# Two batches around a self-attention, staged one behind the other, with the bf16 parts of keys and queries split by GpSimd

## The reference

```python
x = x + _L0_xattn_ref(_layernorm(x, axis=-1), ctx_1024, mask, ...)
x = x + _L0_ffn_ref(_layernorm(x, axis=-1), ...)
...
x = x + _L2_xattn_ref(_layernorm(x, axis=-1), ctx_1024, ...)
x = x + _L2_ffn_ref(_layernorm(x, axis=-1), ...)

def _L0_ffn_ref(hidden_states, ...):     # L2: rmsnorm, no biases, no causal mask
    resid = hidden_states
    x = layer_norm(hidden_states, ln1_w, ln1_b)
    q, k, v = (split(x @ w + b) for each)          # 16 heads of 8
    scores = jnp.where(causal, q @ k.T / sqrt(8), neg)
    ctx = softmax(scores) @ v
    hidden = resid + (ctx @ o_w + o_b)
    xt = layer_norm(hidden, ln2_w, ln2_b)
    logits = xt @ router_w                          # top 2 experts of 16 (L2: of 8)
    return hidden + combine(experts(xt))
```

## Time and profile before

| | us |
|---|---|
| median of 3 runs | 1254.61 (1251.87 to 1260.2) |
| profiled execution, time | 1259.82 |
| profiled execution, span | 1257.6 |
| TensorE busy | 958.8 (76%) |
| VectorE busy | 589.2 (47%) |
| ScalarE busy | 437.1 (35%) |
| GpSimd busy | 218.4 (17%) |

### The profile page before, as it was taken

One profiled execution on the slowest core, in us unless ns is written; L12 is line 12 of the kernel. 1 busy time (PEld: TensorE's weight loads), 2 busy tenths in 40 slices (PEclk: granted clock), 3 DMA queues, 4 the chain that ended last, 5 costly groups with the idle time before them and its releaser, 6 DMA issues. The chain is left out here.

```text
span 1257.6 us, 15487 instructions
## 1 busy us (share of the span) xinstructions
PE 958.8 (76%) x5556; PEld 645.7 (51%) x5561; DVE 589.2 (47%) x1312; ACT 437.1 (35%) x761; POOL 218.4 (17%) x243
## 2 busy tenths in 40 slices
PE   5872599833664638999778925999699988869998
PEld 3661244423653526677647811232266676756776
DVE  4867445351225462311766667576244446632111
ACT  2331155501331203343343310577432233424443
POOL 0334010005033200000372340001000011431100
PEclk9996589965996868999888965799889988989999
DMA  8001511001730000110000006020001111110111
GB/s 343 1 1 48 128 40 40 7 29 39 209 110 9 1 0 1 38 46 17 26 1 1 2 9 167 20 58 2 1 13 38 38 35 51 51 34 18 34 33 34
DMA packets 33264, 55.71 MB, mean 44 GB/s; under 512 B 3697, under 2 KB 25398, under 8 KB 32817
## 3 DMA queue, kind: packets, MB, share of 16 engines
q1 hardware_dynamic: 32176, 52.88, 13.8%
q0 software_dynamic: 1024, 1.98, 0.6%
HBM read 44.81 MB, written 9.96 MB: 44 GB/s over the span
## 5 line engine op out<-in xcount | busy, mean ns | idle before, releaser
L2089 PE MATMUL psum<-xT_all,wexp 128*128 128x512 f32 x400 | 185.1, 608 | 1.3 <-issue 0.7
L1380 DVE TENSOR_REDUCE arena<-psum 128x2 f32<-128x1024 f32 (+3 forms) x128 | 127.6, 1022 | 85.8 <-PE psum L1917 49.9
L949 ACT ACTIVATE arena<-psum 128x512 f32<-128x512 f32 (+3 forms) x256 | 115.8, 515 | 74.9 <-PE psum L1930 37.6
L697 POOL TENSOR_TENSOR rstd<-var,held 128x8 f32<-128x8 f32 (+2 forms) x24 | 51.9, 2180 | 415.8 <-DVE var L1148 392.1
L2089 PEld LDWEIGHTS psum<-xT_all,wexp 128*128 128x128 f32 x400 | 74.6, 196 | 79.1 <-issue 73.2
L1914 PE MATMUL psum<-arena 72*128 72x512 bf16 (+3 forms) x256 | 85.1, 406 | 25.2 <-DMA arena<-parts_q 19.1
L2104 PEld LDWEIGHTS psum<-wexp,arena 128*128 128x128 f32 x800 | 94.2, 192 | 16.2 <-issue 14.4
L1849 PE MATMUL psum<-values_out_all,arena 128*128 128x128 f32 x560 | 78.5, 289 | 26.5 <-ACT arena L921 26.2
L727 POOL TENSOR_TENSOR arena<-arena,small 128x616 f32<-128x616 f32 x56 | 67.9, 1216 | 173.2 <-DVE small L1327 173.1
L2104 PE MATMUL psum<-wexp,arena 128*128 128x128 f32 x800 | 94.7, 275 | 0.9 <-DVE r_res L1619 0.9
L1927 PE MATMUL psum<-arena 75*128 75x512 bf16 (+3 forms) x256 | 77.1, 368 | 13.4 <-DMA arena<-arena 11.5
(11 more groups left out here) (264 smaller groups left out, 1483.9 us busy)
## 6 DMA issues: line engine op xcount, KB each, us to landing
wexp<-experts SPq DMA_DIRECT2D x32, 514.0 KB, 3.5
parts_k<-arena SPq DMA_DIRECT2D x12, 384.0 KB, 3.7
arena<-parts_k SPq DMA_DIRECT2D x48, 96.0 KB
arena<-parts_q SPq DMA_DIRECT2D x48, 96.0 KB
arena<-experts SPq DMA_DIRECT2D x8, 514.0 KB, 3.8
wexp<-experts SPq DMA_DIRECT2D x9, 384.0 KB, 3.1
held<-packed SPq DMA_DIRECT2D x1, 2375.0 KB, 15.4
held<-packed SPq DMA_DIRECT2D x1, 2264.5 KB, 20.8
```

What stands on the lines that cost most here:

```text
L697: pool.tensor_tensor(dst, src, half[0:src.shape[0], 0:n], ALU.pow).then_inc(done, 1)
L949: act.activation(p_self[:, n % 2, kt % 2, j, lo:S], bank(t_bank("keys", c, k), lo, S), ACT.Exp, scale=DS ** -0.5).then_inc(ut_ok, 1)
L1380: dve.tensor_reduce(top[:, x % 2, qt, j:j + 2], src, AX_X, ALU.max, negate=True).then_inc(us_ok, 1)
L2089: mm(bank(c, 0, BANK), wexp[:, side, c * P:(c + 1) * P], xT_all[:, b * S:(b + 1) * S], start=True, stop=True).then_inc(h_ps, 1)
```

## The change

Batch 0's norms, turn and projections are done inside the cross-attention's loop and its drain, at steps counted from `LAST_OF_BATCH` (7). Batch 1's are done in the first ticks of the self-attention, between pairs of batch 0. The buffers for parts, rests and turned tokens hold one batch and lie in wexp and values_out_all; so experts 0 and 1 are loaded by SP behind the stores of batch 1's parts and ahead of the top rows. ScalarE writes the high part and a float32 copy (`k_rest`, `q_rest`); GpSimd makes the middle and low parts of both from it (`split_keys`, `split_queries`) and VectorE's split is gone. The memset of the ring rows is written as float32 (half as many elements) and stands ahead of the cross-attention's loop, behind its token transposes; that of the values is in two, one for each batch. The attention sums of l = 0 and 2 use bank 6 alone; bank 7 serves the turned tokens and k. Each batch's projection, additions, norm, turn and router run in the ticks at 19, 22, 24 and 27 behind its last group, and `moe_input` is left for l = 3 only. SP's order of groups and top rows is as before. Semaphore counts that follow from this are left out here.

```diff
-        U = take(dict(q=8 * S, k=8 * S, P=16 * S, v=NT * HS * 32, o=2 * S, c=NT * P, m=S, top=32, mp=48, rest=16))
+        U = take(dict(P=16 * S, q=8 * S, k=8 * S, v0=TB * HS * 32, top=32, mp=48, rest=16, xn=S, lg=NT * 16, gap=32,
+                      v1=TB * HS * 32, o=2 * S, m=S))
...
-        xn_self, xT_self = U["P"][:, 0:NT * P], U["P"][:, NT * P:2 * NT * P]
-        q_parts, k_parts = (U["P"][:, (4 + 3 * n) * S:(7 + 3 * n) * S].bitcast(BF16).rearrange("p (b n t) -> p b n t", b=B, n=3)
-                            for n in range(2))
-        q_rest, k_rest = (U["P"][:, (10 + 2 * n) * S:(12 + 2 * n) * S].rearrange("p (b t) -> p b t", b=B) for n in range(2))
+        spare = wexp[:, :, :].rearrange("p s n -> p (s n)")
+        k_parts, q_parts = (spare[:, 768 * n:768 * n + 768].bitcast(BF16).rearrange("p (n t) -> p n t", n=3) for n in range(2))
+        k_rest, q_rest, xT_self = spare[:, 1536:2048], values_out_all[:, 0:S], values_out_all[:, S:2 * S]
+        xn_self = U["xn"]
...
+        SELF_AT, MOE_AT = [0, 2, 3], [0, 2, 3, 5]
+        LAST_OF_BATCH = 7
...
-            return 6 if l == 3 else 6 + t % 2
+            return 6 + t % 2 if l == 1 else 6
...
+        def batch_at(tick, after):
+            x = group_at(tick, after)
+            return x // 4 if x is not None and x % 4 == 3 else None
+        def projected_at(tick):
+            return batch_at(tick, 19)
+        def scaled_at(tick):
+            return batch_at(tick, 22)
+        def tokens_turned_at(tick):
+            return batch_at(tick, 24)
+        def routed_at(tick):
+            return batch_at(tick, 27)
...
+                first = 2 * (B * u + b) + 1
+                for n, (k_ready, k_at, q_ready, q_at) in enumerate(((hi_ok, first, hi_ok, first + 1),
+                                                                    (k_split, first, q_split, first),
+                                                                    (k_split, first + 1, q_split, first + 1))):
...
                 store_split(u, 1)
                 split_stored(sp, u, 1)
+                for side in range(2):
+                    if u == 0:
+                        load0(side, side)
+                    else:
+                        load(2, side, side)
                 for x in range(GROUPS):
...
+            def split_keys(u, b):
+                at = B * u + b + 1
+                pool.wait_ge(hi_ok, 2 * at - 1)
+                step.then(pool.tensor_tensor(k_rest, k_rest, k_parts[:, 0, :], ALU.subtract))
+                pool.tensor_copy(k_parts[:, 1, :], k_rest).then_inc(k_split, 1)
+                pool.wait_ge(k_split, 2 * at - 1)
+                step.then(pool.tensor_tensor(k_rest, k_rest, k_parts[:, 1, :], ALU.subtract))
+                pool.tensor_copy(k_parts[:, 2, :], k_rest).then_inc(k_split, 1)
...
+                u = l // 2 if l in (0, 2) else None
+                if u is not None:
+                    pool.wait_ge(x_xTp, 2 * l + 2)
+                    if l == 2:
+                        pool.wait_ge(qrstd_ok, NT)
+                    pool.memset(U["k"][64:96, :], ONES_IN_PAIRS).then_inc(ones_set, 1)
+                    pool.wait_ge(ones_set, u + 1)
...
+                    if u is not None and n == 3:
+                        pool.memset(U["v0"], 1.0).then_inc(wide_set, 1)
+                    if u is not None and n == LAST_OF_BATCH + ADD - 1:
+                        batch_tokens(0, a_stat, SELF_AT[l] + 1, a_rstd)
+                    if u is not None and n == LAST_OF_BATCH + ADD:
+                        batch_tokens(0, b_stat, B * u + 1, b_rstd)
...
+                l = 2 * u
+                split_keys(u, 0)
+                split_queries(u, 0)
+                batch_tokens(1, a_stat, SELF_AT[l] + 2, a_rstd)
+                batch_tokens(1, b_stat, B * u + 2, b_rstd)
+                pool.wait_ge(pT_ps, FIRST_HALF[l] + HALVES[l])
+                pool.memset(U["v1"], 1.0).then_inc(wide_set, 1)
+                split_keys(u, 1)
+                split_queries(u, 1)
...
+                    if x == GROUPS - 1:
+                        batch_tokens(0, m_stat, MOE_AT[l] + 1, m_rstd)
...
+                batch_tokens(1, m_stat, MOE_AT[l] + 2, m_rstd)
...
+                    if l in (0, 2):
+                        if n == LAST_OF_BATCH + 8:
+                            self_tokens(l // 2, 0, 7)
+                        if n == LAST_OF_BATCH + 9:
+                            self_projected(l // 2, 0, 0, 7)
+                        if n == LAST_OF_BATCH + 10:
+                            self_projected(l // 2, 0, 1, 0)
...
+            def self_projected(u, b, which, n):
+                parts, rest, own = ((k_parts, k_rest, "s0_k_b"), (q_parts, q_rest, "s0_q_b"))[which]
+                act.wait_ge(pj_ps, 3 * (B * u + b) + which + 1)
+                if b:
+                    split_stored(act, u, b - 1)
+                func, kw = (ACT.Identity, dict(bias=w(own))) if u == 0 else (ACT.Copy, {})
+                act.activation(parts[:, 0, :], bank(n, 0, BANK), func, **kw)
+                act.activation(rest, bank(n, 0, BANK), func, **kw).then_inc(hi_ok, 1)
...
+                self_tokens(u, 1, 4)
+                self_projected(u, 1, 0, 5)
+                self_projected(u, 1, 1, 6)
...
+                    if u is not None and n == LAST_OF_BATCH + ADD:
+                        self_moments(u, 0)
...
+                    if u is not None:
+                        if n == LAST_OF_BATCH + ADD:
+                            self_residual(u, 0)
+                        if n == LAST_OF_BATCH + ADD + 1:
+                            self_normal(u, 0)
+                        if n == LAST_OF_BATCH + 11:
+                            self_values(u, 0, 1)
...
+            def self_normal(u, b):
+                dve.wait_ge(b_rstd, B * u + b + 1)
+                scaled(xn_self, r_res, rms=(u == 1), done=b_xn, tiles=batch(b), to=b * TB)
...
+                self_moments(u, 1)
+                self_residual(u, 1)
+                self_normal(u, 1)
...
+                def projected(b):
+                    r_, x_ = (v[:, b * S:(b + 1) * S] for v in (r_res, x_res))
+                    dve.wait_ge(us_ps, s_count(u, "project", b))
+                    dve.tensor_tensor(r_, r_, bank(s_bank("project", b), 0, BANK), ALU.add).then_inc(us_ok, 1)
+                    dve.wait_ge(us_ok, s_count(u, "project", b))
+                    if u == 0:
+                        step.then(dve.tensor_tensor(tiles(r_), tiles(r_), wide(w("s0_o_b")), ALU.add))
+                    dve.tensor_tensor(x_, x_, r_, ALU.add)
+                    moments(r_res, m_stat, rms=(u == 1), eps=[EPS_LN, 1e-6][u], tiles=batch(b))
+                def tokens_scaled(b):
+                    dve.wait_ge(m_rstd, MOE_AT[l] + b + 1)
+                    scaled(xn_moe, r_res, rms=(u == 1), done=m_xn, tiles=batch(b))
...
+                        pe.wait_ge(x_done, (1 if l == 1 else 2) + NT * l + t)
...
+                    if l in (0, 2):
+                        if n == LAST_OF_BATCH + 8:
+                            self_turned(l // 2, 0, 7)
+                        if n == LAST_OF_BATCH + 9:
+                            self_projected(l // 2, 0, 0, 7)
+                            pe.wait_ge(e_sub, FIRST_HALF[l] + HALVES[l] - 1)
+                            self_projected(l // 2, 0, 1, 0)
+                            self_projected(l // 2, 0, 2, 1)
                     if n >= VALUE:
...
-                pe.wait_ge(lo_ok, 2 * B * (u + 1))
+                pe.wait_ge(hi_ok, 2 * B * u + 2)
+                pe.wait_ge(v_in_ok, B * u + 1)
+                pe.wait_ge(e_sub, FIRST_HALF[l] + HALVES[l])
...
+                    if tick == 3 - LEAD:
+                        self_turned(u, 1, 4)
+                    if tick == 4 - LEAD:
+                        self_projected(u, 1, 0, 5)
+                        self_projected(u, 1, 1, 6)
+                    if tick == 5 - LEAD:
+                        self_projected(u, 1, 2, 4)
+                    if tick == 8 - LEAD:
+                        pe.wait_ge(hi_ok, 2 * B * (u + 1))
+                        pe.wait_ge(v_in_ok, B * (u + 1))
...
```

333 lines of the change are left out of this document (178 added, 155 removed).

## The result

The changed kernel takes 1213.01 us (median of 4 runs, 1212.67 to 1215.26), the kernel before 1255.46 beside it. The ratio is 0.9663, 95% interval 0.9629 to 0.9698: faster by 42.4 us, where 35 were forecast. The profiled execution took 1213.29 us (span 1211.2) and is 46.5 us shorter than the one before, 4 us more than the medians differ by.

What follows compares the result with a forecast made beforehand. Some 60 us ahead of each self-attention were taken as latency, not work. Stage sums of -16.7 and -18.3 made -35 us, so 1220 us as a median, range 1200 to 1242.

Steps and rivals of the forecast that it cites:

- Part 1: Batch 0's front in the cross-attention's loop and drain: batch 1's x_res 9.7 us later, plus 1.4 in the first stage.
- The blocking of normalisations: In the loop, GpSimd's multiplication holds up VectorE's normalisations, twice: +1.7 us, bounds 0 and 2 x 1.22.
- the term for VectorE's additions and the single bank: In the loop, VectorE's 5.0 us of new work mostly reaches TensorE, as values(10) waits for tile 4's add: 4.5 us.
- the ring's memset: At l = 0 the 4,096-column memset waits for token transposes and delays the first reduction: +1.4 us, first stage only.
- Part 2: From batch 1's x_res to the first exponent: 33.3 us instead of 60.7 and 61.8, saving 27.4 and 28.5.
- loses 1.8 us on the path: Ahead of the first exponent: GpSimd's split ends 5.8 us after q's copy, where VectorE's ended 4.0 after.
- Part 3: Batch 0's projection, norm and router in the steady loop: +4.5 us each, TensorE's 2.6 paid and score banks dry about 2.
- Part 4: The tail to the logits, for one batch instead of two: 4.9 us less in the first stage, 4.0 in the second.
- A: Rival: clock rises sooner after the first score, more if VectorE's loop work is mostly absorbed; total 1204 us, chance 0.17.
- B: Rival: part 1 at 11.5, part 3 at 7, GpSimd's split at its upper end; 1234 us, chance 0.22.
- C: Rival: slower than before, GpSimd's serial split holds the path; gain gone at 3.1 us per operation, 1269 at 4; chance 0.06.
- D: Rival: batch 1's score chain or top row still waits for both batches, first exponent at +50 to +60; about 1250, chance 0.07.

Runs made afterwards that it cites:

- the two edits above: Against the changed kernel: two sum banks for tiles 0 to 4, 1206.5 us; or VectorE's addition of tile 4 ahead of batch 0's normalisation, 1209.35 us.
- the fitted dummies: Changed kernel plus TensorE products that nobody reads, their number fitted to TensorE's waits in each stage: 1208.82 us, ratio 0.9611.
- the two runs with most dummies: Changed kernel plus unread TensorE products fitted to its waits, 1208.82 us; and with more of them, two sum banks and earlier ones for batch 1's values, 1202.01 us.
- the run with the first dummies: Changed kernel plus 25 TensorE products per stage that nobody reads, put into its waits ahead of the steady part: 1213.55 us, ratio 0.9666.

## Why the prediction was right, step by step

The forecast of 1220 was 7 us too high, inside the range, and its mechanism is the one that the trace shows: the way to the first exponent halves, the loop and the steady part pay some of it back. The miss would be smaller by some 2 us without help from the clock, as is said at part 3, and part 1 met its sum in the first stage partly by luck.

**Part 1**, 9.7 us (11.1 in the first stage): 12.0 and 12.1. Behind the eleventh reduction, where the change's work stands, it is 9.6 and 11.4; the rest is 0.7 and 1.7 us in the first stage, a later first reduction and a fall of the clock that is not of the change's making, and 0.7 in the second. So the first stage met the sum partly by luck, for two of its terms missed in opposite directions: the drain took 2.7 us more than before (15.6 for 12.9 from the last reduction to the last addition) and in the second stage 2.6, where 3.5 were forecast, and the loop ahead of it 7.0 and 8.8, where 6.2 were forecast (4.5 and the 1.7 of blocking). The blocking of normalisations, taken at 1.7, is 2 x 0.87 = 1.74. The Trainium skill, "SBUF — State Buffer", section "SBUF: two separate sides", has an exclusive lock for a whole instruction. By an estimate from the rows, three of the four normalisations (0.83 us) behind the end of the multiplication at 76.84 would be 1.1 us more each time, so the trace comes near that rule and stays 0.24 short of it. What was too small is the term for VectorE's additions and the single bank, 4.5: some 5 us in the first stage and 7 in the second, of which 1.5 and 3.8 are the wait that the two edits above remove. That the ring's memset would delay the first reduction by 1.4 is borne out: the product it reads ends at 33.87 and the reduction starts at 35.39, 1.5 us later, behind the memsets. Against the kernel before only 0.7 shows, since that product came 0.7 us earlier in this execution.

**Part 2**, 33.3 us to the first exponent: 30.0 and 31.1. Up to the split's end the sum gave 24.0 and the trace 22.5: a power of four elements took 1.01 us and not the 1.64 of eight, and the normalisation under the memset 2.37 and not 2.9. The split took 7.4 (7.6): its subtractions 1.15 (1.05), its casts 0.61 (0.75). The figure of 769 ns in the Trainium skill, "GPSIMD Engine Reference", section "Performance versus the Vector engine", is above the 0.61 us of this row. Store to issue was 1.7, not 2.8, and the 0.8 us for the experts' bytes did not exist, by the run with these loads behind. Four terms, all on the careful side, make the 3.3 us.
One step of this part failed outright: that GpSimd's split "loses 1.8 us on the path", and that VectorE "has little to do then". With VectorE the first exponent is 3.1 and 2.8 us later, not 1.8 earlier. VectorE has twelve maxima to take there, and the top row waits for the eighth.

**Part 3**, +4.5 each: +1.0 and +1.2, the second of them with help from the clock. The run with both parts undone has the move at 3.5 us there, at the same clock; 2.3 us of that are hidden in the comparison with the kernel before, whose clock was up only 17 us behind the first exponent and not 11 (rows below). So the term was near the mark in the second stage, where TensorE is busy for 103 of 112 us and its 2.6 us are paid. In the first stage the same run has the move at 1.0 us, at least, since its own clock was the lower (0.91, 0.93 in the changed kernel). There the lump of VectorE (203.38 to 207) and TensorE's 2.6 us did not come on top of each other; "2.6 us are paid" took every busy microsecond as path, though that loop leaves TensorE idle for 11 of 100.

**Part 4**, -4.9 and -4.0: -5.6 and -4.5. The size was right and the account was not: moving batch 0 away is worth 2.9 and 2.1, and the rest is there without it.

**Parts 3 and 4 together** were forecast at -0.4 and +0.5, that is nothing, and undoing them moved the time by 1.4 us, within its interval. Against the kernel before they stand at -4.6 and -3.3, which is 8 us of what the forecast missed; 2.3 of it is the clock. By its own account, -35 against -46.5 in the profiled executions, the sum is: parts 3 and 4 8.0 better, part 2 5.4 better, part 1 3.3 worse, 1.4 us elsewhere. As a median it is 7 us, since the profiled execution of before was 5.2 above its median and the one after stands at it.

**The rivals.** A, the clock helps: it fell for the first stage and held in part for the second. In the first stage the 10 us behind the first exponent run at 0.50 in both kernels with the same busy times, to the hundredth for TensorE (9.52 us), and the clock is up 14 us behind the exponent in both. In the second stage it rose 6 us earlier in the changed kernel. Two rows of the kernel before, then the same two of the changed one, from the first exponent on:

```profile
core 0: us, PE busy (x) PEld busy (x) DVE busy (x) ACT busy (x) POOL busy (x), PEclk, DMA share, GB/s
787.60:797.60 10.00, 10.00 (x29) 3.21 (x31) 6.12 (x5) 6.80 (x13) 1.07 (x5) 0.50 0.00 0
797.60:802.60 5.00, 5.00 (x20) 1.17 (x16) 2.10 (x2) 1.78 (x4) 0.00 (x0) 0.50 0.01 2
...
744.30:754.30 10.00, 10.00 (x29) 3.21 (x31) 6.12 (x5) 6.79 (x13) 1.07 (x5) 0.50 0.00 0
754.30:759.30 5.00, 5.00 (x28) 1.26 (x21) 2.51 (x3) 2.33 (x5) 0.00 (x0) 0.87 0.11 33
```

By the run with the queries on VectorE, where it rose at 17 us as before, that is worth 2.7 us (115.2 for 112.5). Whether it comes with the change is open: it rose at 11 to 13 us in nine of the ten profiles without dummies that have the change in them, at 17 in one, and of the kernel before there is one profile. A's own reason failed in any case: the rise did not follow the first score, which stands 25 us ahead of the first exponent in the first stage now and stood 20 ahead before. That the clock could help more is shown by the fitted dummies. B had part 1 right, 11.5 us (12.0 and 12.1 measured), and fell with the steady part (1 us, not 7) and the split (7.4 us, not 10.4). C needed 3.1 us for each split operation; they took 1.15 and 0.61. D fell at the first exponent, 30 us after the last addition.

## What to carry to other kernels

When work is put into a loop that runs in lockstep, look for the short instruction on the same queue that frees a buffer for another engine: an addition of 0.27 us behind a normalisation of 1.97 cost 1.5 to 4 us per stage, and changing places with it was worth as much as a second buffer as far as the profiles tell. Before a difference of a stage is put down to an edit, compare the part of the stage that the edit doesn't touch, and its clock: 1.7 us of one such difference lay there. An engine that looks idle by its busy share may hold the next link of another chain, so moving work to it has to be costed by what stands behind it, not by its idle time. And where a latency-bound stretch feeds a stage bound by TensorE, the clock at the stage's start is a term of its own: 3 us of 101 and 4 of 112 here, gained by filling the waits of the stage ahead, though not in every try.

## What the runs showed of the hardware

VectorE and GpSimd hold each other up in both directions, and for operations that read as well as for memsets. GpSimd's cast took 0.95 us beside VectorE's subtraction and 0.61 alone, VectorE's subtraction 1.34 beside GpSimd's and 0.69 alone; four normalisations took 1.98 under a multiplication and 2.37 under a memset, 1.11 alone. Each time the held-up engine ended 0.1 to 0.5 us earlier than if it had waited for the other's whole instruction. Two engines that halve a job of this kind gain little of the half: the parts were stored by 125.6 us with the split shared and by 126.5 without, of 7.4 us.

The granted clock stayed at 0.50 through the first 10 us of the steady part in every run without dummies, with TensorE busy for 9.5 to 10 of them, and it rose 11 to 17 us behind the first exponent. With the fitted dummies it stayed at 1.00 for the first 43 us of the first stage. In the two runs with most dummies it still fell in the second stage, 1.3 and 5.4 us into the steady part, at or behind idle stretches of 0.9 and 1.1 us; in the run with the first dummies it stayed up behind one of 1.06. No run here explains the difference.
